# Each expert's second product directly behind its own first product

## The reference, cut to what matters

```python
D_MODEL = 256
HIDDEN = 4 * D_MODEL
N_EXPERTS = 8
TOP_K = 2
CAP_FACTOR = 1.0
# fc1_w (8, 256, 1024), fc2_w (8, 1024, 256), biases fc1_b and fc2_b
```

## Time and profile before

| | |
|---|---|
| median of three runs | 1696.94 us (1694.86 to 1700.15) |
| the profiled execution | 1697.25 us |
| its span, first to last instruction | 1695.1 us |
| TensorE busy | 1528.6 us, 90% |
| VectorE busy | 1004.7 us, 59% |
| ScalarE busy | 671.8 us, 40% |
| GpSimd busy | 337.5 us, 20% |
| mean granted TensorE clock | 0.946 |

### The profile page before, as it was taken

One profiled execution on the slowest core, in us unless ns is written; L12 is line 12 of the kernel. 1 busy time (PEld: TensorE's weight loads), 2 busy tenths in 40 slices (PEclk: granted clock), 3 DMA queues, 4 the chain that ended last, 5 costly groups with the idle time before them and its releaser, 6 DMA issues. The chain is left out here.

```text
span 1695.1 us, 20816 instructions
## 1 busy us (share of the span) xinstructions
PE 1528.6 (90%) x7631; PEld 1075.4 (63%) x7631; DVE 1004.7 (59%) x1884; ACT 671.8 (40%) x1292; POOL 337.5 (20%) x249
## 2 busy tenths in 40 slices
PE   7999999999899758979993889899788899989998
PEld 5788888877666424656882355455574555556887
DVE  6777777713323788234444689899345777744444
ACT  1355555501121331202221589797251555533221
POOL 3100000001303102012004159497651000000000
PEclk9999999999999879979996979899889999999999
DMA  5200000043322200013543012122000343101111
GB/s 184 72 19 13 13 19 13 7 124 102 102 62 73 100 1 0 1 66 132 192 143 102 27 50 101 55 95 74 16 1 18 76 103 91 23 1 46 59 60 62
DMA packets 94432, 105.77 MB, mean 62 GB/s; under 512 B 13925, under 2 KB 78041, under 8 KB 94222
## 3 DMA queue, kind: packets, MB, share of 16 engines
q1 hardware_dynamic: 91278, 96.39, 18.5%
q0 software_dynamic: 3072, 8.30, 1.6%
HBM read 83.65 MB, written 14.81 MB: 58 GB/s over the span
## 5 line engine op out<-in xcount | busy, mean ns | idle before, releaser
L976 POOL TENSOR_TENSOR m_state_c<-m_state,m_c 128x1024 f32<-128x1024 f32 x64 | 153.3, 2397 | 87.6 <-DVE m_state L2759 71.3
L2759 DVE TENSOR_TENSOR_SCAN m_state<-m_decay,psum 128x512 f32<-128x512 f32 x128 | 149.0, 1207 | 14.3 <-POOL m_state_c L976 9.7
L2907 DVE TENSOR_REDUCE a_max_pieces<-psum 128x4 f32<-128x512 f32 (+2 forms) x176 | 107.9, 639 | 51.4 <-PE psum L1685 29.8
L2162 ACT ACTIVATE a_probT<-psum 128x512 f32<-128x512 f32 (+1 forms) x176 | 97.2, 558 | 89.2 <-PE psum L1712 85.8
L1553 PE MATMUL psum<-m_state_c,ident 128*128 128x512 f32 x256 | 121.4, 597 | 3.7 <-POOL m_state_c L976 3.7
L1073 PE MATMUL psum<-ones_bf,ident_bf 128*128 128x512 bf16 x375 | 92.5, 405 | 20.6 <-DVE var_eps L2248 4.9
L923 POOL TENSOR_TENSOR rstd<-var_eps,half_neg 128x4 f32<-128x4 f32 x18 | 20.3, 1130 | 427.2 <-DVE var_eps L2248 427.2
L2472 DVE TENSOR_TENSOR f_h<-f_silu,psum 128x512 f32<-128x512 f32 (+1 forms) x46 | 31.5, 686 | 106.1 <-ACT f_silu L1925 91.7
L2093 ACT ACTIVATE m_b_inputT<-m_dtuT,m_bcT 128x256 f32<-128x256 f32 x218 | 93.1, 496 | 1.0 <-PE psum L1545 0.9
L1925 ACT ACTIVATE f_silu<-psum 128x512 f32<-128x512 f32 (+1 forms) x46 | 27.5, 597 | 164.2 <-PE psum L1253 141.5
L1545 PEld LDWEIGHTS psum<-ident,m_b_inputT 128*128 128x128 f32 x512 | 62.1, 151 | 42.6 <-DVE m_state L2759 35.2
(11 more groups left out here) (432 smaller groups left out, 3493.0 us busy)
## 6 DMA issues: line engine op xcount, KB each, us to landing
f_fc<-in_L_ffn_fc_w_dram SPq DMA_DIRECT2D x16, 1024.0 KB, 5.8
m_c<-m_c_rows SPq DMA_DIRECT2D x32, 512.0 KB, 3.6
f_share<-f_share_rows SPq DMA_DIRECT2D x32, 256.0 KB, 3.0
f_out_rows<-f_out SPq DMA_DIRECT2D x16, 256.0 KB, 2.2
f_slot_rows<-f_out SPq DMA_DIRECT2D x1, 2560.0 KB, 9.6
f_rows_in<-f_slot_rows SPq DMA_DIRECT2D x10, 256.0 KB, 3.0
wkv<-in_L_attn_Wk_dram SPq DMA_DIRECT2D x16, 128.0 KB, 2.2
wkv<-in_L_attn_Wv_dram SPq DMA_DIRECT2D x16, 128.0 KB, 2.2
```

The source lines that it names most:

```text
L976: pool.tensor_tensor(hc2[c][:], h2[c][:], c_wide[v][:].rearrange("p (b s) -> p b s", b=BATCH), ALU.mult).then_inc(s_hc, 1)
L2162: act.activation(probT3[n % 2][:, PROB3[i]:PROB3[i] + wide], bank[TURNED3[at % 3]][:, 0:wide], ACT.Exp).then_inc(s_exp3, 1)
L2759: ins = dve.tensor_tensor_scan(h2[c][:, b], dec2[c][:, b], bank[4 + 2 * c + b], 0.0, ALU.mult, ALU.add)
L2907: dve.tensor_reduce(max_of3[n % 2][:, int(diagonal), t_, heads[0]:heads[-1] + 1], o, AX.X, ALU.max).then_inc(s_max3, 1)
```

## The change

TensorE's loop in `experts1` calls `outputs(e)` in round e, where it called `outputs(e - 1)`. Nothing else is different; the lists of the other engines, SyncE's among them, are the same, with their waits.

```diff
                     hidden(e)
                     if e + 1 < EXPERTS1:
                         turn_slots(e + 1)
-                    if e:
-                        outputs(e - 1)
-                outputs(EXPERTS1 - 1)
+                    outputs(e)
```

## The result

The changed kernel takes 1705.59 us (four runs, 1704.25 to 1706.86) against 1696.84 us: ratio 1.0049, interval 1.0032 to 1.0067, slower. The prediction was 1703.1, slower.

A forecast was written before the change was run, and what follows sets the result against it. TensorE, running experts1 without a pause, was taken as the bound. Gelu waits 4.80 + 1.23, expert 0's gain -0.46 and bias additions 0.65 gave about +6.2 us, 1703.1 us; range 1699.3 to 1707.5.

The forecast's parts named there:

- The gelu pauses, experts 1 to 6: TensorE ahead of these second products: 0.72 us waiting for gelu plus 0.08 cold start each, 4.80 us for six.
- Expert 7 and expert 0: Second product 7 waits 1.23 us, having no transposes ahead; at expert 0 the slot copy is hidden, minus 0.46 us.
- The bias additions: Raw blocks requested late delay VectorE's additions for experts 1 and 4; second product 6 waits 0.65 us, product 3 none.
- Rival A: Second products 3 and 6: raw blocks land sooner, no wait for bias additions; +5.6 us, 1702.5; chance 0.20.
- The tail: From last store to TensorE's next projection: chain gains nothing, gap stays 33.3 us.
- Rival B: Projection after the stage: full clock returns earlier, saving about 3 us, total 1699.5 to 1700.1; chance 0.16.
- Rival C: Inside the stage: new pauses make the clock fall, 1.5 us each, 12 after eight, total 1705 to 1715; chance 0.07.

The follow-up runs named there:

- e5: Kernel before in its old order, with one added wait for the next expert's gelu ahead of each second product; 1704.61 us, ratio 1.0039.
- e2: Changed kernel with SyncE asking for first weights e + 2 behind first product e, so no request waits for the next expert; 1704.78 us, ratio 1.0038.
- e0: Kernel before, timed and profiled again without any edit; 1699.09 us, ratio 1.0010.
- e3: Changed kernel with two edits: second products wait by gelu pair, and SyncE's weight requests in order; 1696.88 us, ratio 0.9994.
- e1: Changed kernel with the second product waiting for each gelu pair just ahead of the blocks that need it, not for all four; 1706.23 us, ratio 1.0040.
- e6: Changed kernel with the transposes of expert e + 1 behind second product e, not ahead of it; 1715.65 us, ratio 1.0104.
- e7: e1 with ten short filler matmuls ahead of second products 3 and 6; 1703.41 us, ratio 1.0031 against the kernel before.
- e4: Changed kernel, timed and profiled again without any edit; 1704.99 us, ratio 1.0038.

## Why the prediction was right, point by point

**The gelu pauses, experts 1 to 6.** Forecast 0.72 and 0.08 each. Measured at expert 2: 8.05 - 7.34 = 0.71, and from the second product to the next start 828.87 - 821.89 = 6.98 where 6.91 stood, 0.07. Right, and e5 shows that the wait is the cause.

**Expert 7 and expert 0.** Forecast 1.23 and -0.46. Measured 897.58 - 889.54 - 6.91 = 1.13, with the slower start behind a pause 1.20; and 791.79 - 783.62 = 8.17 against 789.71 - 781.11 = 8.60, -0.43. Right. (Where the prediction lists the second products, one term too many stands in its line, the 6.99; its times 804.3, 819.35 and 834.4 are the sums without it, and product 3 would by the gelu alone have come at 834.4 + 2.51 = 836.9: measured 837.10 with 0.18 for VectorE.)

**The bias additions.** The term of 0.65, all at product 6. In the profile it is divided: from first to second product 8.23 us at product 3 and 8.41 at product 6, where 8.05 is the gelu alone, so 0.18 and 0.36, 0.54 together; e2 takes away 0.55. The two starts of the quantisation, forecast for a stage that begins at 781.11, came 0.36 later and 0.2 earlier than forecast after the shift of 2.51 us of the whole stage. The mechanism was right and its price inside the bounds (0 to 1.3), but the division was not: the prediction gave the two blocks 12.37 and 13.21 us from the first weights request to the start of quantisation (8.72 + 3.65, 8.72 + 4.49), and they took 12.70 (818.57 - 805.87) and 12.82 (864.01 - 851.19). That the sum came so near is partly luck, for the two errors lean against each other. Rival A, no wait for the bias additions, is out: TensorE did wait for VectorE. By the rule of the Trainium skill (SBUF — State Buffer, "The DMA setup-cost knee") the prediction had estimated 9.8 us from the first of the four requests to the last landing. The traces do not agree with it: the raw blocks took 11.1 and 11.3 us from their own issue, which is 12.7 and 12.8 from the first request (805.87 and 851.19).

```profile
DMA to landing us min/median/max: 11.1/11.2/11.3
```

**The tail.** Forecast unchanged, 33.3 us from store to TensorE's return: 33.26.

**The clock.** Rival B, that the clock gives something back behind the stage, happened in the profiled execution of the change: its first projection output was copied 8.39 us after TensorE's return, 10.57 in the kernel before. But e0, the same kernel as before, had 8.39 too, e2 10.27 and e3 10.73. It belongs to executions, not to the change. In the same way the clock had fallen ahead of the stage in the profile of the change (granted 0.50 from 780 to 782 us, behind a pause of 1.74) and made it begin later:

```profile
778.42 3.61 PE L1073 MATMUL psum<-ones_bf,ident_bf 128*128 128x512 bf16 x10 [1.74 <-issue]
```

```profile
780.00:781.00 1.00, 1.00 (x4) 0.32 (x3) 0.00 (x0) 0.00 (x0) 0.00 (x0) 0.50 0.09 30
```

With the start at +2.51, the stage at +6.03 and the rest at -1.5 the span's difference of 7.1 is complete. Rival C, a fall inside the stage, did not happen in the change (pauses of 0.54 to 0.97 us, clock 1.00) and did in e1, at 1.7 us each where the prediction had 1.5. The Trainium skill (TensorE: Matmul & The Clock Gate, "A second HAM failure mode: psum-queue depth-cycling"; the prediction names the section ahead of it) says that frequent short idle times between groups of matmuls made the clock go back and forth between its two levels. In the sixteen pauses of up to 1.02 us in e6 that was not seen. The falls in e1 stood behind two longer pauses, of 1.93 and 2.75 us. But ahead of the stage of e7 the clock fell, and the longest pause of the 20 us before was 0.34:

```profile
780.85 3.42 PE L1073 MATMUL psum<-ones_bf,ident_bf 128*128 128x512 bf16 x8 [0.34 <-issue]
```

```profile
782.00:783.00 1.00, 1.00 (x4) 0.38 (x3) 0.00 (x0) 0.00 (x0) 0.00 (x0) 0.50 0.39 136
```

In e1 and e4 the same row of four pauses of 0.31 to 0.34 us stood there, and the granted clock stayed at 1.00. So the length of the last pause does not decide alone, and that no fall came in the change is what was measured, not something that these runs promise.

What was sized a little low is the total: 1703.1 forecast, 1705.59 and 1704.99 measured. The stage explains 6.0 of the 8.7 and 6.8 us, and 1.0036, the ratio that it makes, lies in both intervals. The remainder has no cause shown. By their ratios, all kernels of the table but e1 lie 0.2 to 2.4 us further above the kernel before than their stages do, and e0, in which nothing is changed, 1.7 us; so about as much appears without the change. The start of the stage differs by up to 7.8 us over the ten profiled executions.

## What to carry to other kernels

An order that puts a consumer one item behind its producer hides the other engine's work between them; here, taking the consumer next to its producer cost the latency of that work once for each item, however small it is against the items, unless the consumer's waits are as fine as the producer's outputs. When one engine's order is changed, walk the lists of the engines that wait for it in their own order: here requests for data that no one had touched went out late, and removing only the visible pause uncovered them. For a change of a few microseconds measure the stage inside one execution; the total needed many runs to say the same less well.

## What the runs showed of the hardware that was not expected

Inside the stage, pauses of TensorE of 0.5 to 1.0 us left the granted clock at 1.00 in all ten profiles, also when sixteen of them stood in 130 us (e6). Pauses of 1.93 and 2.75 us (e1) were each followed by about 3.4 us at the lower clock, which cost 1.7 us beside the pause, and ten filler matmuls (2.3 us) in the pause avoided it (e7). Ahead of the stage it was less regular: behind a pause of 1.74 us the clock fell (the change), behind 1.44 (before) and 1.25 (e2) it did not, and in e7 it fell behind pauses of no more than 0.34.

Requests in company landed later: the first raw block took 6.0 us when it was asked for behind a store alone and second weights 2.8 us before (e2), and 11.1 us in the change, behind two blocks of weights and a store, all asked for within 2 us.

Two executions of the same program began the stage 7.8 us apart (781.11 and 788.94); they were already 8.5 us apart at a row of filler matmuls 50 us earlier (730.81 and 739.33).
